# Six projections of the next tile in three adjacent pairs, and ScalarE's copies of values behind the squares of their pair

## The reference, cut to what matters

```python
def attn_layer(x, Wqkv, qs, ksc, Wo):
    q, k, v = jnp.split(x @ Wqkv, 3, -1)          # 16 heads of 64
    q = l2norm(q) * qs
    k = l2norm(k) * ksc
    q = q * cos * scale + rotate_half(q) * sin * scale
    k = k * cos * inv + rotate_half(k) * sin * inv
    out = local_attention(q, k, v)                # window of 32: softmax(q k^T) v
    return out @ Wo

for i in range(DEPTH):                            # DEPTH = 6
    x = attn_layer(shift_tokens(x), ...) + x
    x = ffn_layer(shift_tokens(x), ...) + x
```

## Time and profile before

| | us |
|---|---|
| median of 3 runs | 2512.28 |
| lowest and highest of them | 2510.72, 2596.46 |
| the profiled execution | 2513.5 |
| its span in the profile | 2511.7 |
| busy in the span: PE, DVE, ACT, POOL | 2084.1 (83%), 1743.5 (69%), 1632.6 (65%), 1740.9 (69%) |
| mean granted clock of TensorE, full speed being 1 | 0.966 |

### The profile page before, as it was taken

One profiled execution on the slowest core, in us unless ns is written; L12 is line 12 of the kernel. 1 busy time (PEld: TensorE's weight loads), 2 busy tenths in 40 slices (PEclk: granted clock), 3 DMA queues, 4 the chain that ended last, 5 costly groups with the idle time before them and its releaser, 6 DMA issues.

```text
span 2511.7 us, 70965 instructions
## 1 busy us (share of the span) xinstructions
PE 2084.1 (83%) x23552; PEld 1533.5 (61%) x23552; DVE 1743.5 (69%) x4197; ACT 1632.6 (65%) x5654; POOL 1740.9 (69%) x1364
## 2 busy tenths in 40 slices
PE   6999478888888888888888888888788888888886
PEld 4666356666566666466666466665466665566663
DVE  4555667777667777577776777775777776777764
ACT  3555257767567777577776577776577775777772
POOL 4333468888578787588885788885788885888860
PEclk9999779999999999999999999999999999999998
DMA  1000111111021111111111121111211110111110
GB/s 61 1 0 0 43 53 49 40 38 38 22 75 40 46 40 39 53 45 38 38 48 33 54 50 40 38 39 34 63 41 47 39 38 22 48 44 44 38 37 17
DMA packets 40902, 98.65 MB, mean 39 GB/s; under 512 B 6480, under 2 KB 20432, under 8 KB 39856
## 3 DMA queue, kind: packets, MB, share of 16 engines
q1 hardware_dynamic: 40752, 96.75, 14.9%
HBM read 20.32 MB, written 1.05 MB: 9 GB/s over the span
## 4 chain that ended last, share of the span: by engine, by line
PE 39%; issue 19%; DVE 17%; ACT 15%; POOL 8%; DVEq 1%; POOLq 0%; ACTq 0%; DMA 0%; SPq 0%
ACT prob L478 10%; PE bank L1201 5%; PE bank L1146 5%; DVE nmax L748 3%; PE bank L1193 3%; PE bank L1187 3%; DVE ts_ L801 3%; PE bank L1137 3%; DVE o_nat L758 2%; PE bank L1180 2%; ACT qT L516 2%; POOL tsum L319 2%; PE bank L1182 2%; PE bank L1181 2%; PE bank L1050 2%
## 5 line engine op out<-in xcount | busy, mean ns | idle before, releaser
L317 POOL TENSOR_TENSOR rn<-n2c,half_neg 128x8 f32<-128x8 f32 x384 | 632.9, 1648 | 351.0 <-DVE n2c L798 341.8
L478 ACT ACTIVATE prob<-bank,nmax 128x96 f32<-128x96 f32 x1536 | 508.7, 360 | 401.9 <-DVE nmax L748 401.7
L319 POOL TENSOR_TENSOR tsum<-tc_,ts_ 128x512 f32<-128x512 f32 x384 | 493.3, 1285 | 0.0
L1153 PE MATMUL bank<-idf,prob 128*96 128x128 f32 x1536 | 247.2, 285 | 241.6 <-ACT prob L478 241.6
L322 POOL TENSOR_TENSOR w_nat<-tsum,rn 128x512 f32<-128x512 f32 x384 | 401.0, 1044 | 37.8 <-POOL tsum L319 15.1
L791 DVE TENSOR_REDUCE n<-nat 128x8 f32<-128x512 f32 x384 | 261.3, 680 | 188.9 <-ACT nat L494 122.3
L478 ACT ACTIVATION_READ_ACCUMULATOR prob<-bank,nmax 128x1 f32 x1536 | 347.0, 226 | 0.0
L1153 PEld LDWEIGHTS bank<-idf,prob 128*96 128x96 f32 x1536 | 152.9, 128 | 301.1 <-issue 288.6
L1180 PE MATMUL bank<-w_hi,xs 128*128 128x512 f32 x576 | 288.9, 502 | 9.5 <-DVE ts_ L801 7.0
L801 DVE TENSOR_TENSOR ts_<-bank,ropeL 128x256 f32<-128x256 f32 x768 | 285.8, 412 | 0.0
L748 DVE TENSOR_REDUCE nmax<-bank 128x4 f32<-128x384 f32 x384 | 196.1, 552 | 125.5 <-PE bank L1146 117.6
(11 more groups left out here) (129 smaller groups left out, 3988.1 us busy)
## 6 DMA issues: line engine op xcount, KB each, us to landing
vspace<-v_nat SPq DMA_DIRECT2D x96, 384.0 KB, 4.0
vspace<-v_nat SPq DMA_DIRECT2D x96, 256.0 KB, 3.5
vspace<-v_nat SPq DMA_DIRECT2D x95, 128.0 KB, 2.3
nat<-w_qkv SPq DMA_DIRECT2D x5, 1536.0 KB, 7.8
wo<-w_o SPq DMA_DIRECT2D x6, 512.0 KB, 4.0
w<-w SPq DMA_DIRECT2D x6, 341.0 KB, 3.0
shared<-w_qkv SPq DMA_DIRECT2D x1, 1536.0 KB, 6.6
w<-w SPq DMA_DIRECT2D x6, 192.0 KB, 3.0
```

What stands on the lines that cost most here:

```text
L317: nc.gpsimd.tensor_tensor(rn[:, r, :], n2c[:, r, :], half_neg[:, 0:8], ALU.pow).then_inc(pool_step, 1)
L319: nc.gpsimd.tensor_tensor(tsum[:, r, :], tc_[:, r, :], ts_[:, r, :], ALU.add).then_inc(pool_step, 1)
L478: last = nc.scalar.activation(prob[:, 4 * b + i, :], SB[b][:, i * SPAN:(i + 1) * SPAN], ACT.Exp, bias=nmax[:, p, 8 * G + 4 * b + i:8 * G + ...
L1153: last = nc.tensor.transpose(RING[at][0:SPAN, i * P:(i + 1) * P], prob[:, 4 * b + i, :], idf[:, :])
```

## The change

On TensorE, projection 1 moves from behind the turn of heads 2 to directly behind projection 0; projection 3 moves from behind `scores(t, n, p, 1)` to directly behind projection 2, ahead of the turn of heads 3, `project_out` of the tile before and these scores; projection 5 moves from behind the turn of the output to directly behind projection 4. On ScalarE, `values(t + 1, 1 - p, 0)` moves from behind the exponentials `exps(t, p, 1, 0)` to directly behind `square(t + 1, 2)`, ahead of `heads_T(t, p, 3, 4)`; `values(t + 1, 1 - p, 1)` moves from behind `heads_out_T(t, 0, 4)` to ahead of it. No instruction, wait or count is added or removed, and VectorE, GpSimd and SyncE are as before.

```diff
 # TensorE, tile()
                     else:
                         project(t + 1, 1 - p, 0)
+                        project(t + 1, 1 - p, 1)
...
                     transpose_heads(t, 2, 6 if opening else 4)
                     if closing:
                         transpose_in(1)
-                    else:
-                        project(t + 1, 1 - p, 1)
...
                     if not closing:
                         project(t + 1, 1 - p, 2)
+                        project(t + 1, 1 - p, 3)
                     eng.wait_ge(pt_evac, t * 4 + (1 if opening else 2))
                     transpose_heads(t, 3, 4)
                     if not opening:
                         project_out(t - 1, 1)
                     scores(t, n, p, 1)
-                    if not closing:
-                        project(t + 1, 1 - p, 3)
...
                     if not closing:
                         project(t + 1, 1 - p, 4)
+                        project(t + 1, 1 - p, 5)
                     eng.wait_ge(pt_evac, t * 4 + 3)
                     transpose_out(t, 0, 4)
-                    if not closing:
-                        project(t + 1, 1 - p, 5)
 # ScalarE, tile()
                     if not closing:
                         square(t + 1, 2)
+                        values(t + 1, 1 - p, 0)
                     heads_T(t, p, 3, 4)
                     exps(t, p, 1, 0)
...
-                        values(t + 1, 1 - p, 0)
                         heads_T(t + 1, 1 - p, 0, 6)
...
                         square(t + 1, 3)
+                        values(t + 1, 1 - p, 1)
                     heads_out_T(t, 0, 4)
...
-                        values(t + 1, 1 - p, 1)
                         heads_T(t + 1, 1 - p, 1, 6)
```

## The result

The changed kernel took 2685.8 us (median; 2679.93 to 2689.95) against 2513.0 for the kernel before: a ratio of 1.068, 95% interval 1.063 to 1.073. Predicted were 2690 us, between 2625 and 2755. That the total came so near is in part luck: the last pair was priced too high, the first tiles and the clock too low. Two readings behind the sum were wrong as well, which engine ends the second half of a tile and what sets the end of rotary 1.

The account below looks back on a forecast made before the run. Bound: a ring passed twice a tile (scores, maxima, exponentials, transposes, ScalarE's copy of heads). 1.77 + 0.10 = 1.87 us a tile, times 90 = 168 us; with 10 us for the clock 2690 us, range 2625 to 2755.

Parts of the forecast that it names:

- Projection 1: nothing: First half: the turn of heads 2 ends 0.79 us later, but ScalarE fetches it later still; no cost.
- Projection 3, +1.77 us: First half: projection 3 waits about 1 us for rotary 1 to release its bank, delaying the scores by 1.77 us.
- Values 0 out of the second half, -0.47: Second half: without this ScalarE copy, TensorE's second turn of probabilities starts 0.47 us earlier.
- Projection 5 and values 1, +0.57: Second half, behind the turn of probabilities: heads_out_T and project_out come later, the scores by 0.57 us.
- In the second half TensorE is last: End of the second half: scores follow project_out's start by 1.20 us, ScalarE's last copy having ended earlier.
- The case named with the +0.10: Second half: if the 0.3 us between project_out's issue and the scores hides, it gains 0.2 us instead of losing 0.10.
- First tiles at the same price: First and last tiles of each layer were taken to lose the same 1.87 us as the others.
- Clock, 10 us: TensorE's clock: the added gaps bring seven more falls to the lower level, 10 us in all.
- Rival 1: Second half gains its whole 0.47 us, leaving 1.30 us lost a tile; 2630 us, chance 0.10.
- Rival 3: Rotary 1 ends earlier, projection 3 doesn't wait; the first half still loses 0.72 us; 2587 us, chance 0.05.
- Rival 2: TensorE's clock falls in every second tile, adding 68 us; 2750 us, chance 0.14.
- Rival 4: Not slower: ScalarE's work sets the pace, only values 0's 0.47 us counts; 2471 us, chance 0.03.

Follow-up runs that it names:

- e_first: Kernel before with only projection 1 moved to directly behind projection 0; ratio 1.000.
- e_mid: Kernel before with only projection 3 directly behind projection 2 and values 0 behind square 2; 2649.1 us, ratio 1.059.
- e_late: Kernel before with ScalarE's values 0 moved behind exps(t,p,1,1) and its input copy behind heads_T(t,p,3,4); 2455.2 us, ratio 0.977.
- e_last: Kernel before with only projection 5 directly behind projection 4 and values 1 ahead of heads_out_T; 2533.7 us, ratio 1.010.
- e_fill: Changed kernel with projection 2's three matmuls made twice, to fill the gap before projection 3; 2679.5 us.
- e_clamp: Changed kernel with VectorE's L794 left out of rotary 1 and that rotary's clamp of the norms moved behind L801; 2661.1 us, ratio 1.057.
- e_late_p2: As e_late, with projection 2 also moved ahead of transpose_out(t - 1, 1, 6) on TensorE; 2427.2 us, ratio 0.966 to the kernel before.

## Why the prediction was right, and where it wasn't

- **Projection 1: nothing.** Right (e_first).
- **Projection 3, +1.77 us.** Right in mechanism and nearly in size: 1.85 in the mean. The missing 0.08 is on ScalarE's side, which was put at 0.07 less than TensorE's and came last: the values copy started 1.16 us behind projection 3 (1231.43 to 1232.59) instead of 1.01. Wrong was the step that "none of what leads to it moves" because rotary 1 stands "directly behind VectorE's other work": the rotary's end is held up by GpSimd's sum as well, which stretches the clamp by 0.25 us here. The row for it, the clamp of 0.41 us, was in the trace and not asked after. The number survived by luck: the same sum stood at the same place in both kernels.
- **Values 0 out of the second half, -0.47.** Right: 0.49 in e_mid and in e_late.
- **Projection 5 and values 1, +0.57.** Mis-sized: +0.29 (e_last), and the step that failed is "In the second half TensorE is last". Of the 1.20 us from `project_out`'s start to the scores only 1.00 is TensorE's; in the other 0.20 it waited for ScalarE's copy to `kT` and passed the waits behind it. In the changed kernel the product is later than that copy, and the scores follow it by 1.00. The case named with the +0.10 has this number but another reason, an issue gap. Another 0.10 is that `heads_out_T` came at P + 2.55, not 2.65. The second half thus became 0.19 shorter instead of 0.10 longer.
- **First tiles at the same price.** Mis-sized: their first halves alone cost 2.75 us each (16.5 / 6) where a whole tile was put at 1.87. Why is open.
- **Clock, 10 us.** Twelve more slow halves, 17 us; seven were assumed. The denser gaps were the argument, and e_fill did not bear it out.
- **Rivals.** Rival 1 (the second half gives back its whole 0.47) didn't happen with the last pair in place; e_mid without it shows just that. Rival 3, a projection 3 that needn't wait: e_clamp has that state but for 0.05 us, 10.49 against 9.56, a loss of 0.93 where 0.72 was worked out; from projection 3 to the scores it took 2.30 us (1225.65 to 1227.95), not 2.14. Rival 2's falls in every second tile didn't come. Rival 4 is out: the first half's slip came through whole. Its condition was wrong too: by rival 3's own sum an earlier rotary leaves 0.72, more than the 0.47 that the second half returns.

The sum before the clock said 168 us; the halves gave 156 - 16 + 16.5 = 157. The clock's 17 us instead of 10 closed most of the rest, which was luck: the reason given for the clock's term did not hold.

## What to carry to other kernels

When work is moved forward on an in-order engine, price the wait it meets there and everything queued behind it, from the rows of what releases it: here 0.9 us of waiting (11.41 to 10.49 in e_clamp) and 0.9 of work ahead of the scores (10.49 to 9.56), in 90 tiles. Two adjacent uses of a pair of banks put the second use's wait for its bank ahead of work that had none. One projection moved into an existing wait gained 28 us, and one copy of ScalarE's moved off its stretch ahead of the turn 57; together 3.4%. When two engines' work ends close together ahead of a step, look for idle time in front of it: 0.2 us of a wait had been taken for issue here. And before a wait is ascribed to an engine's own work, look at the lengths of its small operations: one that is several times its usual length is itself waiting.

## What was not expected of the hardware

A VectorE operation on 128x8 elements took from 0.16 to 0.90 us in the rows shown, depending on where in GpSimd's 1.29 us sum it began, and taking 0.68 us of VectorE's work out ahead of it gained nothing. In e_late and e_late_p2, which differ from the kernel before only in order, none of the 168 halves of tiles 1 to 14 was slow, against seven.
